# State-space stage of a four-layer image block on one core: stacked 3x3 taps, group 0 prepared beside attention, and an order written out per iteration

## The chip, the cores and the metric

The kernel runs on one core of one Trainium2 chip. The metric is device time in microseconds (us) of one execution. Five engines run their own instruction streams and meet at semaphores: TensorE (PE), VectorE (DVE), ScalarE (ACT), GpSimd (POOL) and SyncE (SP), which issues DMAs.

## The reference

Input and output are float32 images of 16 x 28 x 28 x 32. Four residual layers, each on a normalised image: window attention, a state-space layer, a triangle product, a recurrence. The change lies in the second:

```
x1 = grouped_1x1(gn(x), w1);  x1 = silu(conv3x3_depthwise(x1, dw))        # SAME padding
u, z = x1 @ in_proj                                                      # over the sequence of 784 pixels
u = silu(up[0:L]*c[0] + up[1:L+1]*c[1] + up[2:L+2]*c[2] + bias)          # causal, 3 taps
dt, B, C = x_proj(u);  delta = softplus(dt @ dt_proj + bias)
h_t = exp(delta_t * A[n]) * h_{t-1} + delta_t * u_t * B_t[n];  y = sum_n C_t[n] * h_t   # n = 0..7
y = (y + u * D) * silu(z);  x1 = layernorm(y @ out_proj) * gamma + beta
x = x + grouped_1x1(x1 * silu(grouped_1x1(gn(x), w2)), wout)
```

## The kernel before, in words

The image lies in X with 128 partitions, four images by 32 channels, and J = 4 groups of 784 columns (T = 784, HT = 392 a half). Weights are spread into block diagonals BD[128 x 128] for the four images (spread_weights, L1185). The 3x3 convolution is folded with w1 into nine such taps, U_CV.

Attention goes through 16 strips of 196 columns, software-pipelined over 18 steps: pe_att, act_att, dve_att and pool_att (L761, L547, L1230, L405), with steps 3 to 14 in hardware loops. dve_att(s) adds the projection of strip s-2 to X (L1253, semaphore x1_r). A strip takes 7.2 to 7.4 us.

Then gn_stats(1) and gn_apply(1) normalise all groups into XN, here with a border (30 x 30 a group), and the state stage starts. SSM_STEPS are six iterations i = -2 to 5. In iteration i each engine handles group f = i+2 (convolution, S1, u, z, x2), k = i+1 (delta, softplus, x_B, x_C), c = i (the eight states), m = i-1 (output, variance) and w = i-2 (scale, product wout, residual). The states of c:

- PE (pe_ssm): spread("B", n) and spread("C", n), L907, copy row n of B or C to all channels in PSUM, from three bf16 pieces in BCf. spread B n waits for the scan n-1 (v_s), spread C n for times_c(n-1) (v_c), since each has a single result place, pairs[0] and pairs[1]. All other products go to pairs[2] and pairs[3]; claim() waits until the last result there is read. conv is 18 full matmuls of 392 columns (L921), cut into pieces between the spreads; inner (L935) has 6.
- ACT (act_ssm): dA[n] = exp(A[n] * DL), L627, in four buffers, softplus in small steps in sp (L638 to L672), copies out of PSUM, and Silu. Functions of different tables need an ACT_TABLE_LOAD between them.
- DVE (dve_ssm): slot(n) is times_b (L1308), scan (L1315) and times_c(n-1) (L1328). DU = DL * US is L1380; y1 and y2 (L1362, L1367) make the gated output; L1350 shifts, L1373 is the residual.
- POOL (pool_ssm): add(n), L452, sums the eight hC into YA; split() (L460, L462) makes the bf16 pieces of B and C; L481 to L496 end the softplus in DL; L501 and L468 work on the layer norm.

Every engine works in program order, and waits are on semaphores: p_<name> that a product is there, c_<name> that it is read, v_dl, v_du, a_da, g_ya and so on. Engines reach the iterations in the same order, but nothing else ties them. In iteration -2 and -1 DVE has only DU of group 0 to do. While conv of group 0 runs, DVE prepares weights of the later layers (L1284 to L1299). After iteration 5 come gn_stats(2), gn_apply(2) and the triangle layer, then the recurrence.

## Time and profile before

| | us |
|---|---|
| median of 3 runs | 547.66 (546.55 to 547.82) |
| profiled execution | 548.09 |
| its span | 546.6 |
| PE busy | 387.7 (71%) |
| DVE busy | 373.4 (68%) |
| ACT busy | 289.5 (53%) |
| POOL busy | 229.6 (42%) |

Times in views are from the start of the span. The stages in it: loading and setup to 37, attention to 161, preparation of the state stage to 212, its four full iterations to 362, its tail to 393, triangle layer to about 470, recurrence to the end. A busy share is a mean over these; it says what bounds a stage only where the waits of that stage are read with it. PEclk is the granted TensorE clock, 1.00 for 2.4 GHz and 0.50 for 1.2 GHz.

### The profile page before, as it was taken

What the parts mean: (1) busy time and instruction counts of PE and PEld (TensorE: products, weight loads), DVE (VectorE), ACT (ScalarE), POOL (GpSimd) and SP (SyncE); (2) the same over time, 40 slices, a digit from 0 to 9 for tenths busy, and PEclk for the clock granted to TensorE, in tenths of its full rate; (3) what the DMA queues carried; (4) which work ended last, traced back from release to release, by engine and by line L of the source; (5) the groups of instructions that cost most, each with busy time, mean ns of one, the idle gap of its engine ahead of it and who ended that gap; (6) DMA issues with size and microseconds to landing.
All of it is one profiled execution on the core that took longest, in us unless ns stands there. A gap on an engine that the chain in (4) does not pass through costs nothing. (4 is left out here: it accounts for less than half of the span.)

```text
span 546.6 us, 10366 instructions
## 1 busy us (share of the span) xinstructions
PE 387.7 (71%) x3674; PEld 261.8 (48%) x3674; DVE 373.4 (68%) x679; ACT 289.5 (53%) x545; POOL 229.6 (42%) x205
## 2 busy tenths in 40 slices
PE   4169888899848898997995625423496181988885
PEld 3046666667635454453552201101385141987775
DVE  3797988888865003989988989974445776554443
ACT  4226888888850476837765720505476621333333
POOL 3616666777640090694795793483042000000000
PEclk9999999999997999898996755858597575999999
DMA  5100000000000000000000000000000000011111
GB/s 128 9 12 1 2 1 0 0 0 0 2 1 0 0 2 0 0 1 0 1 1 0 0 0 1 1 1 1 0 1 2 2 0 0 14 22 21 20 20 23
DMA packets 21571, 3.98 MB, mean 7 GB/s; under 512 B 19752, under 2 KB 21544, under 8 KB 21544
## 3 DMA queue, kind: packets, MB, share of 16 engines
q1 hardware_dynamic: 21416, 3.61, 4.0%
q8 instruction: 17, 0.28, 0.2%
q0 software_dynamic: 128, 0.01, 0.1%
q14 instruction: 10, 0.08, 0.1%
HBM read 2.00 MB, written 1.61 MB: 7 GB/s over the span
## 5 line engine op out<-in xcount | busy, mean ns | idle before, releaser
L452 POOL TENSOR_TENSOR YA<-YA,hC 128x784 f32<-128x784 f32 x28 | 53.7, 1919 | 42.2 <-DVE hC L1328 41.7
L425 POOL TENSOR_TENSOR Pr<-Pr,rc 128x392 f32<-128x392 f32 x64 | 52.3, 849 | 44.0 <-DVE rc L1263 44.0
L907 PE MATMUL pair<-BCf,sel 96*128 96x392 bf16 x128 | 39.8, 408 | 41.1 <-DVE Hs L1315 32.7
L1315 DVE TENSOR_TENSOR_SCAN Hs<-dA,pair 128x784 f32<-128x784 f32 x32 | 57.2, 1786 | 2.9 <-ACT dA L627 1.9
L921 PE MATMUL pair<-XN,BD 128*128 128x392 f32 x144 | 52.4, 513 | 5.9 <-DVE XN L1174 4.8
L907 PEld LDWEIGHTS pair<-BCf,sel 96*128 96x128 bf16 x128 | 11.0, 105 | 74.4 <-issue 71.7
L1241 DVE TENSOR_REDUCE mx<-pair 128x8 f32<-128x392 f32 x64 | 33.1, 558 | 14.0 <-PE pair L782 14.0
L570 ACT ACTIVATE PT<-pair 128x512 f32<-128x512 f32 x64 | 37.9, 592 | 7.9 <-PE pair L824 7.7
L921 PEld LDWEIGHTS pair<-XN,BD 128*128 128x128 f32 x144 | 28.0, 198 | 25.8 <-issue 9.8
L824 PE MATMUL pair<-ident,Pr 128*128 128x128 f32 x256 | 37.3, 285 | 3.5 <-POOL Pr L425 3.3
L1308 DVE TENSOR_TENSOR pair<-DU,pair 128x784 f32<-128x784 f32 x32 | 31.2, 974 | 10.6 <-PE pair L907 10.1
L576 ACT ACTIVATE Pr<-Ts 128x392 f32<-128x392 f32 x64 | 34.5, 541 | 5.6 <-DVE Ts L1247 4.9
L1380 DVE TENSOR_TENSOR DU<-DL,US 128x784 f32<-128x784 f32 x4 | 8.8, 2193 | 39.2 <-POOL DL L496 39.2
L782 PE MATMUL pair<-Km,Qw 32*64 32x196 f32 x512 | 31.3, 363 | 4.8 <-DVE Ts L1247 2.7
L824 PEld LDWEIGHTS pair<-ident,Pr 128*128 128x128 f32 x256 | 30.7, 146 | 8.2 <-POOL Pr L425 5.0
L1077 PE MATMUL pair<-XN,BD 128*128 (+1 forms) x168 | 25.5, 290 | 12.0 <-DVE XN L1174 12.0
L627 ACT ACTIVATE dA<-DL,Aneg 128x784 f32<-128x784 f32 x32 | 28.4, 938 | 9.3 <-POOL DL L496 9.3
L1089 PE MATMUL pair<-hst,BD 128*128 128x112 f32 x168 | 26.3, 294 | 9.4 <-DVE hst L1473 8.5
L1247 DVE TENSOR_TENSOR Ts<-pair,mx 128x392 f32<-128x392 f32 x64 | 32.9, 556 | 0.0
L1259 DVE TENSOR_REDUCE sm<-Pr 128x8 f32<-128x392 f32 x64 | 31.8, 539 | 0.0
L732 ACT ACTIVATE gates<-pair 128x224 f32<-128x224 f32 x28 | 10.0, 357 | 39.1 <-PE pair L1089 39.1
L460 POOL TENSOR_TENSOR BCf<-BCf 64x784 f32<-64x784 f32 x8 | 11.9, 1486 | 44.4 <-ACT BCf L644 44.4
(201 smaller groups left out, 944.9 us busy)
## 6 DMA issues: line engine op xcount, KB each, us to landing
XT<-in_x SPq DMA_DIRECT2D x4, 392.0 KB, 5.7
out<-Os SPq DMA_DIRECT2D x28, 56.0 KB, 1.8
NB<-in_L_conv_x_proj_w SPq DMA_DIRECT2D x4, 3.0 KB
DW<-in_L_conv_dw SPq DMA_DIRECT2D x4, 1.1 KB
vec<-in_L_conv_b_qkv POOLq DMA_DIRECT2D x3, 0.5 KB, 6.5
W<-in_L_conv_w_qkv SPq DMA_DIRECT2D x1, 48.0 KB
BL<-in_L_conv_bi SPq DMA_DIRECT2D x3, 0.5 KB
BL<-in_L_conv_bf SPq DMA_DIRECT2D x3, 0.5 KB
```

The lines of the kernel that those rows point to most:

```text
L425: eng.tensor_tensor(pg, pg, bcast(rc[:, g, :], 2, WT), ALU.mult).then_inc(pn_r, 1)
L452: eng.tensor_tensor(y, y, hC[:, n % NHC, :], ALU.add).then_inc(g_ya, 1)
L570: eng.activation(PT[:, g].rearrange("p a b q -> p (a b q)"), banks[5 + (par + 1 + g) % 2][:, :], ACT.Copy).then_inc(ring_r, 1)
L576: eng.activation(Pr[:, par, g, :, 0:WT], Ts[:, g, :, :], ACT.Exp).then_inc(exp_r, 1)
L782: ins = eng.matmul(banks[g][64 * half:64 * half + 64, 196 * pair:196 * pair + 196], Qw[C * g:C * g + C, par, 2 * pair + half, :], Km[C * g ...
L824: ins = eng.transpose(bk[:, P * k:P * k + P], pg, ident[:, :])
L907: ins = eng.matmul(SPREAD[s][:, HT * h:HT * h + HT], sel[:, n, :], upper(BCf[:, c % 2, s, HT * h:HT * h + HT]), start=True, stop=True)
L921: ins = eng.matmul(result("conv")[:, h, :].rearrange("p (y x) -> p y x", x=W), BD[:, U_CV + tap, :], img[:, f, y:y + 14, x:x + W], start=( ...
L1241: eng.tensor_reduce(mx[:, g, :], banks[g][:, 0:392].rearrange("p (m k) -> p m k", k=WT), AX.X, ALU.max).then_inc(max_r, 1)
L1247: eng.tensor_tensor(Ts[:, g, :, :], banks[g][:, 0:392].rearrange("p (m k) -> p m k", k=WT), bcast(mx[:, g, :], 2, WT), ALU.subtract).then_ ...
L1259: eng.tensor_reduce(sm[:, g, :], Pr[:, par, g, :, 0:WT], AX.X, ALU.add).then_inc(sum_r, 1)
L1315: eng.tensor_tensor_scan(Hs[:, n % 2, :], dA[:, n % NA, :], SPREAD[0], 0.0, ALU.mult, ALU.add).then_inc(v_s, 1)
```

## The change

What is computed stays. (1) The 3x3 taps: a normalised group lies in XP (two buffers, bordered). SP copies it by 12 DMAs of 32 partitions to SX, where three copies shifted by 0, 1 and 2 columns are stacked in 96 partitions for each of the four images. A half of the convolution is then 3 rows x 4 images of matmuls, 96 deep and 32 wide, with W3, in place of nine of 128 x 128. (2) Groups 0 and 1 are normalised within attention (after strip steps 10 and 12, which are unrolled on ACT and DVE), group 2 and 3 within iterations 0 and 1. (3) Group 0's convolution, u, delta and softplus are placed between the last steps of attention on PE, ACT, DVE; its results use pairs[0] and [1] (LEAD). The convolution, u and delta are handed on in halves. (4) Iterations run from 0 to 5, each with its order written out, for each engine; S1 has two buffers; y1 and y2 share yz, nt has one buffer instead of three, SP_W shares SP_U. (5) selections() moves from setup to step 15 of attention, later_weights() to iteration 4.

```diff
-        XN = sb("XN", [P, J * 30 * 30])
-        BD = sb("BD", [P, NU, P])
+        XN = sb("XN", [P, N])
+        XP = sb("XP", [P, 2, 30 * 30])
+        SX = sb("SX", [3 * C, G, 30 * 30])
+        W3 = sb("W3", [3 * C, 3, C])
+        BD = sb("BD", [P, U_CV, P])
...
+        LEAD = dict(conv=0, u=0, delta=1, xB=0, xC=1)
...
+            for b in range(J):
+                eng.wait_ge(xp_r, b + 1)
+                if b:
+                    eng.wait_ge(p_["conv"], count("conv", b - 1))
+                for x in range(3):
+                    for g in range(G):
+                        eng.dma_start(SX[C * x:C * x + C, g, 0:898], XP[C * g:C * g + C, b % 2, x:x + 898]).then_inc(s_sx, 16)
...
+            act_att(11, 1)
+            gn_ln(0, 2, 1)
+            gn_exp(0, 2)
+            for s in (12, 13, 14, 15):
+                act_att(s, s % 2)
...
+            silu_conv(0, 0)
+            silu_conv(0, 1)
+            def begin():
+                silu_u(0, 0)
+                silu_u(0, 1)
+                sp_abs(0, 0)
+                sp_abs(0, 1)
+            act_att(16, 0, begin)
+            sp_e(0)
+            sp_relu(0)
+            copy_bc(0, 0, "xB")
+            sp_u(0)
+            sp_l(0)
+            gn_ln(2, 3, 2)
+            copy_bc(0, 1, "xC")
+            sp_w(0)
+            gn_exp(2, 3)
+            silu_z(0)
+            silu_conv(1, 0)
+            silu_conv(1, 1)
+            decays(0, 0, 1, 2, 3)
...
+                elif i == 1:
+                    sp_abs(2, 0)
+                    sp_abs(2, 1)
+                    sp_relu(2)
+                    sp_e(2)
+                    sp_u(2)
+                    sp_u1(2)
+                    decays(1, 4)
+                    copy_bc(2, 0, "xB")
+                    decays(1, 5)
+                    sp_l(2)
+                    out_m(0)
+                    sp_w(2)
+                    copy_bc(2, 1, "xC")
+                    decays(1, 6)
+                    silu_conv(3, 0)
+                    silu_conv(3, 1)
+                    var_ln(0)
+                    decays(1, 7)
+                    var_exp(0)
+                    decays(2, 0, 1)
...
+            def conv(b, h):
...
+                for y in range(3):
+                    for g in range(G):
+                        ins = eng.matmul(row_groups(pairs[place("conv", b)][:, :, 0:HT], h)[g], W3[:, y, :],
+                                         rows[:, g, 14 * h + y:14 * h + y + 14, 0:W], start=(y == 0), stop=(y == 2))
...
+            conv(0, 0)
+            conv(0, 1)
+            pe_att(16, 0, early, late)
+            product("xB", 0, WBC[:, 0, :], US[:, 0, :])
+            pe_att(17, 1)
+            product("xC", 0, WBC[:, 1, :], US[:, 0, :])
+            gate(0)
+            conv(1, 0)
+            conv(1, 1)
...
+                if i == 0:
+                    spread("B", 0)
+                    spread("C", 0)
+                    inner(1, 0)
+                    inner(1, 1)
+                    spread("B", 1)
+                    x2(0)
+                    delta(1, 0)
+                    delta(1, 1)
+                    spread("B", 2)
+                    spread("C", 1)
+                    x_b(1)
+                    spread("B", 3)
+                    x_c(1)
+                    spread("C", 2)
+                    gate(1)
+                    spread("B", 4)
+                    spread("C", 3)
+                    conv(2, 0)
+                    spread("B", 5)
+                    spread("C", 4)
+                    conv(2, 1)
+                    spread("B", 6)
...
+            block_stats(0, 1)
+            dve_att(11, 1)
+            dve_att(12, 0)
+            padded(0, 1)
+            padded(1, 1)
+            for s in (13, 14, 15):
                 dve_att(s, s % 2)
+            selections()
+            dve_att(16, 0)
+            block_stats(2)
+            mk, rest = sp[:, SP_M, :], sp[:, SP_C, :]
+            eng.wait_ge(a_u, 1)
+            eng.scalar_tensor_tensor(rest, sp[:, SP_U, :], 1.0, sp[:, SP_E, :], ALU.subtract, ALU.subtract).then_inc(v_cc, 1)
+            dve_att(17, 1)
...
+                elif c is not None:
+                    slot(0)
+                    if i == 1:
+                        padded(3, 3)
+                    if i == 2:
+                        shift()
+                    outputs()
+                    slot(1)
+                    times_c(0)
+                    slot(2)
+                    times_c(1)
+                    slot(3)
+                    times_c(2)
+                    if i == 3:
+                        shift()
+                    slot(4)
+                    times_c(3)
+                    slot(5)
+                    times_c(4)
+                    if i == 2:
+                        residual()
+                    if i == 1:
+                        delta_u()
+                    slot(6)
+                    times_c(5)
+                    if i == 2:
+                        delta_u()
+                    slot(7)
+                    times_c(6)
+                    times_c(7)
+                    if i == 3:
+                        residual()
+                elif i == J:
+                    shift()
+                    outputs()
+                    later_weights()
+                    residual()
```

POOL's order in the changed kernel, which the diff writes out in the same way: iteration 0 is add 1, split(1, B), remainder (the former L481), add 2, plus_log (L486), add 3, delta (L491, L496), split(1, C), adds 4 to 7; iteration 1 is remainder, plus_log, add 1, split(2, B), add 2, delta, split(2, C), adds 3 and 4, scaled (L501), adds 5 to 7; iteration 2 is remainder, gated (L468), split(3, B), plus_log, add 1, delta, split(3, C), adds 2 to 4, scaled, adds 5 to 7; iteration 3 is add 1, gated, adds 2 and 3, scaled, adds 4 to 7. In iteration 4 PE has out_m, wout_w, var_m.

## Rows read from the trace of the kernel before

**Rows 1.** Stage windows: stretch, length, busy us per engine, PEclk, DMA share, GB/s.
```profile
60.00:150.00 90.00, 80.03 (x1486) 61.38 (x1484) 79.01 (x184) 75.20 (x184) 62.26 (x75) 1.00 0.00 1
212.50:249.40 36.90, 33.31 (x109) 16.56 (x107) 31.45 (x25) 25.47 (x29) 24.15 (x14) 0.95 0.00 0
249.40:288.00 38.60, 33.48 (x108) 17.14 (x108) 34.63 (x29) 26.78 (x31) 28.70 (x17) 0.96 0.00 1
288.00:327.90 39.90, 21.09 (x48) 7.08 (x48) 35.47 (x30) 21.20 (x25) 30.37 (x18) 0.61 0.00 0
327.90:362.30 34.40, 16.43 (x42) 4.71 (x42) 31.68 (x29) 9.22 (x10) 16.43 (x9) 0.65 0.00 1
```

**Rows 2.** Groups by line, DVE, 212:363: shapes, count, busy us, mean ns, idle before.
```profile
L1315 DVE TENSOR_TENSOR_SCAN Hs<-dA,pair 128x784 f32<-128x784 f32 x32 | 57.2, 1786 | 2.9 <-ACT dA L627 1.9
L1308 DVE TENSOR_TENSOR pair<-DU,pair 128x784 f32<-128x784 f32 x32 | 31.2, 974 | 10.6 <-PE pair L907 10.1
L1328 DVE TENSOR_TENSOR hC<-Hs,pair 128x784 f32<-128x784 f32 x28 | 26.6, 952 | 1.9 <-PE pair L907 1.8
L1380 DVE TENSOR_TENSOR DU<-DL,US 128x784 f32<-128x784 f32 x3 | 7.8, 2599 | 5.5 <-POOL DL L496 5.5
```

**Rows 3.** Timeline, head of the state stage: start us, us, engine, line, [idle before].
```profile
164.57 2.48 DVE L1174 TENSOR_SCALAR XN<-X,mv,rstd 128x784 f32<-128x784 f32 x4 [1.99 <-ACT rstd L539]
...
182.26 4.19 PE L935 MATMUL pair<-S,BD 128*128 128x392 f32 x12 [1.02 <-ACT S L681]
...
193.47 12.09 PE L921 MATMUL pair<-XN,BD 128*128 128x392 f32 x36 [1.00 <-ACT BCf L644]
...
205.68 0.98 DVE L1380 TENSOR_TENSOR DU<-DL,US 128x784 f32<-128x784 f32 x1 [33.70 <-POOL DL L496]
...
215.38 1.79 DVE L1315 TENSOR_TENSOR_SCAN Hs<-dA,pair 128x784 f32<-128x784 f32 x1 [1.86 <-ACT dA L627]
```

**Rows 4.** Timeline, last strips of attention.
```profile
152.53 0.90 PE L835 MATMUL pair<-PT,Vst 128*32 128x49 f32 x64 [1.28 <-ACT PT L570]
...
154.42 1.91 DVE L1152 BATCH_NORM_STATS2 stats<-X 128x6 f32<-128x392 f32 x4
...
160.64 0.42 DVE L1253 SCALAR_TENSOR_TENSOR X<-pair,vec,X 128x196 f32<-128x196 f32 x1 [2.66 <-PE pair L806]
```

**Rows 5.** Timeline, ACT and POOL in group 0's softplus.
```profile
193.35 1.28 ACT L647 ACT_TABLE_LOAD   x1
...
194.64 0.86 ACT L647 ACTIVATE sp<-sp 128x784 f32<-128x784 f32 x1
...
201.78 1.84 POOL L491 TENSOR_TENSOR sp<-sp 128x784 f32<-128x784 f32 x1 [0.32 <-ACT sp L672]
```

**Rows 6.** Timeline, DVE at the end of setup.
```profile
30.35 2.42 DVE L1185 TENSOR_TENSOR BD<-W,bd 128x2176 f32<-128x2176 f32 x1
...
33.30 3.35 DVE L1221 CAST sel<-ident 32x1024 bf16<-32x1024 f32 x3
...
37.01 1.04 DVE L1241 TENSOR_REDUCE mx<-pair 128x8 f32<-128x392 f32 x2
```

**Rows 7.** Waits, 60:150: who, for whom, us in total, times, longest.
```profile
DVE mx L1241 <- PE pair L782: 10.6, 18, 0.8
```

**Rows 8.** Timeline, SP's queue in setup.
```profile
24.70 0.53 SPq L299 DMA_DIRECT2D W<-in_L_conv_Wox  x1
```

**Rows 9.** DMA issues: count, KB each, median us to landing.
```profile
out<-Os SPq DMA_DIRECT2D x28, 56.0 KB, 1.8
```

**Rows 10.** Timeline, DVE's preparation of later weights, first and last instruction.
```profile
166.97 0.15 DVE L1286 TENSOR_SCALAR vec<-vec 128x1 f32<-128x1 f32 x1
...
171.40 0.58 DVE L1299 TENSOR_TENSOR WZ<-wzs,maskz 64x128 f32<-64x128 f32 x2
```

**Rows 11.** Timeline, DVE in the tail of the state stage.
```profile
374.57 0.97 DVE L1373 TENSOR_TENSOR X<-X,pair 128x784 f32<-128x784 f32 x1 [6.35 <-PE pair L891]
```

**Rows 12.** Timeline, PE in iteration 3, a product.
```profile
337.37 2.98 PE L891 MATMUL pair<-y,BD 128*128 128x392 f32 x4 [1.05 <-DVE y L1367]
```

More of the change, by code:

```diff
@@ new lines, in silu_z, with silu_x2, sp_abs @@
+            def silu_z(b):
+                eng.wait_ge(p_["z"], b + 1)
+                eng.activation(halves(ZS[:, b, :]), result("z", b), ACT.Silu).then_inc(c_["z"], 1)
+            def silu_x2(b):
+                eng.wait_ge(p_["x2"], b + 1)
+                eng.activation(halves(X2[:, b, :]), result("x2", b), ACT.Silu).then_inc(c_["x2"], 1)
+            def sp_abs(k, h):
+                eng.wait_ge(p_["delta"], 2 * k + h + 1)
+                if k and h == 0:
+                    eng.wait_ge(v_dl, k)
+                eng.activation(sp[:, SP_E, columns(h)], result("delta", k)[:, h, :], ACT.Abs, bias=vec[:, V_DTB:V_DTB + 1]).then_inc(c_["delta"], 1)
@@ L888, in product @@
-            def product(name, w, rhs):
-                claim(name)
+                    n, d = last[-1]
+                    if not (d == b and (n, name) in (("conv", "u"), ("u", "delta"))):
+                        eng.wait_ge(c_[n], count(n, d))
+                    if n == "delta":
+                        eng.wait_ge(a_m, d + 1)
+                elif place(name, b) >= 2:
+                    eng.wait_ge(ring_r, 6 * NS)
+                    eng.wait_ge((x1_r, ao_r)[place(name, b) - 2], NS)
@@ L955, in pe_ssm @@
-                spread("B", 3)
-                conv(4, 6)
-                spread("C", 2)
-                if w is not None:
-                    eng.wait_ge(g_nt2, w + 1)
-                    product("wout", BD[:, U_WO, :], nt[:, 2, :])
-                conv(6, 8)
-                spread("B", 4)
-                conv(8, 11)
-                spread("C", 3)
-                if m is not None:
-                    eng.wait_ge(c_["out"], m + 1)
-                    product("var", VB[:, :], sq[:, :])
```

836 lines of the change are left out of this document (537 added, 299 removed).

## The prediction

> **What bounds the kernel now.** First read the stage windows [rows 1], busy time per engine, then PEclk. In the four iterations of the state stage (212.5 to 362.3 us, 149.8 us) DVE works 31.5 of 36.9, 34.6 of 38.6, 35.5 of 39.9 and 31.7 of 34.4 us. PE looks as busy in the first two, but that is work DVE does not wait for: the groups of DVE's instructions [rows 2] show 10.1 us of waiting for the spreads over 32 products, 1.9 us for dA, 5.5 us for DL. So there DVE is the bound. One state needs L1308, L1315 and L1328: 0.97 + 1.79 + 0.95, starts 3.57 us apart when nothing waits, 28.6 us per group.
>
> Second, read the timeline ahead of it [rows 3]. DVE's last instruction of attention is at 160.6 [rows 4]; the first DU is at 205.68 after 33.70 us idle, and the first scan at 215.38. These 54 us are one chain through group 0: statistics, 36 records of the 3x3 convolution at a cold clock, S1, u, delta, softplus, DL, and then group 1's convolution (12.09 us at 193.47) standing on PE in front of the first spread. That head is the largest thing that can be removed.
>
> **The head of the state stage.** Eighteen full-array matmuls take 12.09 us, 0.67 each [rows 3]. The new conv has 12 matmuls a half, each 32 columns wide and 96 rows deep, four of them to different column groups. The nearest row is L835 [rows 4]: 64 records, 32 matmuls on 128*32 tiles, 49 columns, in 0.90 us; at 0.67 us for 392 columns one such matmul alone would take 0.084, 32 of them 2.7. So at least three run side by side. A half then costs between 3 x 0.67 = 2.0 and 8.0/3 = 2.7 us; I take 2.0, as the 0.90 contains start and end.
> The Trainium skill (TensorE: Matmul & The Clock Gate, Measured speedup vs the span model) reports 2.38 times for three column tiles, which at four would make a half 2.5 us by proportion; the sum would lose about 1 us. The row decides for the full overlap, and 2.7 stays the upper end.
>
> Now walk the new order, on the clock of the old trace. PE finishes the av at 152.53 + 0.90 = 153.4 [rows 4]. conv(0,0) and (0,1) end at 155.6 and 157.6. ACT has the Silu table loaded (1.28, [rows 5]) by 155.3, S1 by 156.2 and 158.1. pe_att(16) with inner in it: inner has 3 matmuls a half (12 records took 4.19, [rows 3]), so 2.1 each; transposes, inner(0,0), project, transposes, inner(0,1) end at 164.8, delta(0,1) at 166.3, av(15) at 167.2. ACT: AO at 167.9, table load and sp_e 170.1, relu and xB copy 171.8, sp_u 172.6, table load and sp_l 174.8, xC copy and small Ln 175.8, table load and sp_w 178.1, table load, silu_z and silu_conv(1) 181.3, table load and dA(0) 183.5 (each full-width operation about 0.86, [rows 5]). DVE in parallel: L1253 of the last strip now waits behind a_u and runs at 173.7 instead of 160.6, mk and rest end 179.8 (one may stand behind a POOL split), DL 180.8, DU 181.8, times_b 182.8. conv(1) waits for x1_r 16, 174.2 to 178.2, and spread B 0 follows in time. The first scan starts at 183.5 instead of 215.4: -31.9 us. Unknown: ACT alone carries four table loads between AO and dA, so any slip on it counts fully; bounds -28 and -33.
>
> **Attention and setup.** selections() leaves setup: L1221 cost 3.35 and stood directly before the first L1241 at 37.01, and L1185 shrinks from 2176 to 1024 columns, 2.42 to about 1.2 [rows 6]; W3 and split copies cost about 0.7. Some 4 us less ahead of the first maximum, but Km and the cold PE are close behind; I take -3 (bounds -4 and -1). In the drain the selections stand where DVE now idles, and cost nothing; if the cover were gone, 3.7. Into the steady part go two groups of statistics (1.91, [rows 4]) plus aggregation, two padded (0.62 each as a quarter of the 2.48 of L1174, [rows 3], possibly behind a POOL multiply), and on ACT two tiny operations with two table loads, 3 us. DVE has 10.6 us of waits in 90 us [rows 7], 0.9 a strip, to swallow them; behind each stand maxima and exponentials that PE and POOL wait for. I take +4.5 (bounds +1 and +8). Net +1.5. The memset of XP, half of what XN's was, falls into POOL's idle time (62.3 busy of 90, [rows 1]).
>
> **The 12 copies a group.** SP issues a DMA in 0.53 and every 0.57 us [rows 8]; 12 give 6.8, and the last lands some 1.8 after its issue as the 56 KB stores do [rows 9]: 8.6 us. Group 0 has more than three strips of attention to hide them, group 1 from 157.6 to 174.2. Group 2 can start only after padded(2), near 190, and PE reaches conv(2,0) near 199: just hidden. Group 3: 220 to 231, hidden. SP's queue holds nothing else until the stores of the last stage. Upper bound for a transfer, if 32 partitions take half the rate: 17 us.
>
> **The four iterations.** DVE per group keeps 28.6. Iteration 0 (from scan 0, was 34.0): 27.6 + padded 1.3 + group 3's statistics 1.2 + DU 2.6 (mean of L1380, [rows 2]: 0.98 alone at 205.68, [rows 3], and 2.6 in the loop, beside a POOL operation of 1.84, [rows 5]) + 1.5 of small waits = 34.2, no gain. Iteration 1 (38.6): outputs() now lies between scan 0 and times_b 1 and so covers the 1.0 us wait for the spread, the 1.7 wait for DL changes into one of about 1.9, since POOL does remainder, plus_log, add, split, add, delta in a row (1.84 each), padded costs 1.3, DU lands on POOL less surely: 37.6. Iteration 2 (39.9): DL two us earlier, slot 1 covered, shift without a POOL neighbour: 36.6. Iteration 3 (34.4): the shift (1.3) enters, residual and slot waits leave: 32.9. Sum -5.8 (bounds +4 and -12; each saving is a fraction of a wait, each of the twelve SBUF-only DVE operations may cost 1.6 more or less). conv leaves PE 8 us a group that nobody waited for in iterations 0 and 1: nothing directly. ACT in iteration 1 has, counted in the new order, 24 us of operations (27 or so of 0.86 and halves of it) and nine table loads, 11.5: 35.4 of 37.6. It is nearly a second bound, but dA(4) to dA(7) come out several us before their scans when I walk it, so I cost it at nothing; without that cover 2 to 6 us.
>
> **The tail.** later_weights (166.97 to 171.98, [rows 10]: 5.0 us) moves behind the last outputs(). There DVE idled 6.35 us in front of L1373 (374.57, [rows 11]), and wout now follows out on PE at once, so the residual comes out level or a little earlier: -0.5. If the cover fails, residual(2) is late, and with it var, Ln, rstd: +1. Everything behind is unchanged.
>
> **Sum.** -31.9 + 1.5 - 5.8 - 0.5 = -36.7. The profiled execution took 548.1 (span 546.6 and 1.5 around it), so 511.4; the median of the runs shown is 0.4 lower: 511.0.
>
> **Rivals.** (a) Column groups do not overlap for 392-column streams (four different moving reads at once). Then a half costs 8.0: 12 us more in the chain of group 0, 8.5 for group 1 (2 x 6 less 3.6 of slack before spread B 0), 6 for each of four halves in the loop where the spread behind has 2.1 us of room, 24: 555.5, slower than before. It decides the sign only if a half costs over 7.1 us, an overlap under 1.15; L835's row speaks against. 0.04.
> (b) The clock. Rows 1 show 0.95 and 0.96 in iterations 0 and 1 and 0.61 and 0.65 in 2 and 3, where PE had little to do; a product of two halves at the low level took 2.98 us [rows 12], where two matmuls at 0.67 [rows 3] make 1.34. Without 8 us of convolution, iterations 0 and 1 might run at 1.2 GHz as well: conv and inner halves of 4 us in front of spreads with 2.1 us of room, seven times 1.9, 13 us: 524. For: PE's work falls to 33.5 - 12.1 + 4.0, 25 of 38 us. Against: attention holds 1.00 with pauses in every strip. 0.14. The Trainium skill (TensorE: Matmul & The Clock Gate, HAM oscillation — how this bites in real kernels) warns that pauses between bursts throw the clock back; the granted clock behind the 1.0 us waits of iteration 3 agrees.
> (c) The copies take 17 us each group: conv(2,0) 8 late, conv(3,0) 6 late, PE stands and with it the spreads: 525. 0.09.
> (d) In-order ACT becomes the bound of iterations 0 and 1, or attention stretches by the full 8: 517 to 520. 0.13.
> (e) No DVE and POOL collisions and no DL wait: -12 in the loop: 504.8. 0.10.
> The forecast, 506 to 516, keeps 0.50.
>
> **Range and chances.** 503 to 526 takes in (b) to (e) with their edges and leaves out (a) and the tails of both sides. About 0.3% is what a measurement can tell from no change; all cases but (a) are far beyond it: faster 0.95, same 0.01, slower 0.04.
>
> **What would show it.** First scan between 180 and 188 us; the wait of DVE on DL ahead of the state stage gone from 33.7 to a few us; 24 conv records of a half within 2.0 to 2.7 us; iterations of 33 to 38 us with DVE busy over 0.93; PEclk near 1.0 in the first two; attention's last strip 1 to 3 us later in the stretch before the drain; L1373's counterpart after later_weights at the same distance from the last outputs(). Wrong it would be if a convolution half costs over 4, if PE waits for SP's copies in the loop, or if spreads wait behind products of 3 us.

## The result, and the profile after

| | before | after |
|---|---|---|
| median of the runs, us | 547.11 (4 runs, 546.47 to 547.82) | 523.57 (4 runs, 521.22 to 526.34) |
| ratio after to before | | 0.957, 95% interval 0.952 to 0.962 |
| profiled execution, us | 548.1, span 546.6 | 523.5, span 521.7 |
| first scan of the state stage | 215.38 | 183.46 |
| end of the last times_c of iteration 3 | 362.29 | 333.16 |
| first write of XR | 390.66 | 368.02 |
| from there to the end of the span | 155.9 | 153.7 |

The change makes the kernel 23.5 us faster. The forecast was 511.0 with a range of 503 to 526: the direction and the range held, but the time lies outside the 506 to 516 that were given a chance of one half, and a third of the expected gain is missing. The table tells in which stretch it went. Up to the first scan 31.9 us are gained, against 31.9 - 1.5 = 30.4 expected. From there to the end of the four iterations before took 146.9 us and after takes 149.7: a loss of 2.8 where a gain of 5.8 was forecast. From there to XR before took 28.4 and after 34.9: a loss of 6.5 where a gain of 0.5 was forecast. These two stretches, 8.6 and 7.0 us off, are what the experiments are about.

The stage windows of after, one for each iteration, answer to [rows 1] (stretch, length, busy us of each engine, PEclk, DMA share, GB/s):

```profile
183.40:217.90 34.50, 28.34 (x121) 11.47 (x119) 31.64 (x29) 30.50 (x38) 23.81 (x14) 0.90 0.18 41
217.90:259.20 41.30, 32.51 (x121) 13.34 (x122) 33.44 (x29) 30.44 (x36) 29.26 (x17) 0.79 0.15 34
259.20:299.60 40.40, 22.70 (x63) 8.48 (x61) 33.79 (x30) 28.23 (x33) 30.45 (x18) 0.79 0.00 1
299.60:333.10 33.50, 17.43 (x42) 6.14 (x42) 31.33 (x29) 10.16 (x11) 16.48 (x9) 0.65 0.00 0
```

DVE works 31.6 of 34.5 and 31.3 of 33.5 us in the first and the last, but only 33.4 of 41.3 and 33.8 of 40.4 in the two between: 14.5 us in which the engine that should be the bound stands. The groups of DVE's instructions, 183.4 to 333.2 us, say behind whom; they answer to [rows 2]:

```profile
L1705 DVE TENSOR_TENSOR_SCAN Hs<-dA,pair 128x784 f32<-128x784 f32 x32 | 57.2, 1786 | 1.1
L1698 DVE TENSOR_TENSOR pair<-DU,pair 128x784 f32<-128x784 f32 x32 | 31.1, 973 | 3.7 <-PE pair L1198 3.0
L1718 DVE TENSOR_TENSOR hC<-Hs,pair 128x784 f32<-128x784 f32 x28 | 26.6, 950 | 14.5 <-PE pair L1198 14.5
L1753 DVE TENSOR_TENSOR DU<-DL,US 128x784 f32<-128x784 f32 x3 | 6.5, 2182 | 0.0
```

The three instructions of a state cost what they did. The 5.5 us of waiting for DL are gone, and in front of the scans only 1.1 is left. But in front of times_c there are 14.5 us of waiting for L1198, the spreads, and a spread is a short product that stands in PE's queue behind something else. So the question is what stood ahead of it.

The head came as walked. PE, then DVE, from the timeline of after, beside [rows 3, 4]:

```profile
154.55 4.14 PE L1130 MATMUL pair<-SX,W 96*32 96x392 f32 x48
```

```profile
172.71 1.62 DVE L1658 SCALAR_TENSOR_TENSOR sp<-sp 128x784 f32<-128x784 f32 x1 [8.60 <-ACT sp L746]
...
183.46 1.79 DVE L1705 TENSOR_TENSOR_SCAN Hs<-dA,pair 128x784 f32<-128x784 f32 x1
```

The line of PE is both halves of group 0's convolution, 24 matmuls (two records each) in 4.14 us: 2.07 a half, where 2.0 was taken. Group 1's two halves take 4.16 us from 174.81 on. DVE's longest idle time in the head is 8.60 us in front of the first remainder, waiting for ACT; the scan comes at 183.46.

### The profile page after: what moved, and what is told of

The parts are those of the page before. It is cut to its first block, busy times and chain, and to the rows that moved or that the text cites. A ratio compares the mean times of both kernels' runs of the same rounds, so it can differ in the third digit from the quotient of the medians.

```text
span 521.7 us, 10477 instructions
## 1 busy us (share of the span) xinstructions
PE 365.1 (70%) x3722; PEld 242.5 (46%) x3722; DVE 385.2 (74%) x687; ACT 304.9 (58%) x571; POOL 224.7 (43%) x201
## 4 chain that ended last, share of the span: by engine, by line
DVE 29%; PE 26%; ACT 19%; issue 15%; SPq 5%; POOL 4%; DMA 1%; DVEq 1%; POOLq 0%; ACTq 0%
PE pair L1435 4%; DVE pair L1698 4%; DVE Hs L1705 3%; PE pair L993 3%; SPq L317 3%; PE pair L1130 3%; DVE Ts L1599 2%; PE pair L1198 2%; PE pair L1046 2%; ACT PT L647 2%; PE pair L1114 2%; POOL Pr L451 2%; DVE hC L1718 2%; ACT gates L943 2%; POOL pp L591 1%
## 5 line engine op out<-in xcount | busy, mean ns | idle before, releaser
L451 POOL TENSOR_TENSOR Pr<-Pr,rc 128x392 f32<-128x392 f32 x64 | 54.3, 880 | 41.3 <-DVE rc L1615 41.3
L1198 PE MATMUL pair<-BCf,sel 96*128 96x392 bf16 x128 | 38.5, 405 | 33.1 <-DVE Hs L1705 26.2
L1593 DVE TENSOR_REDUCE mx<-pair 128x8 f32<-128x392 f32 x64 | 32.9, 555 | 14.6 <-PE pair L993 14.6
L1198 PEld LDWEIGHTS pair<-BCf,sel 96*128 96x128 bf16 x128 | 10.7, 106 | 69.2 <-issue 67.0
L647 ACT ACTIVATE PT<-pair 128x512 f32<-128x512 f32 x64 | 37.7, 592 | 7.9 <-PE pair L1035 7.6
L1718 DVE TENSOR_TENSOR hC<-Hs,pair 128x784 f32<-128x784 f32 x28 | 26.6, 950 | 14.5 <-PE pair L1198 14.5
L653 ACT ACTIVATE Pr<-Ts 128x392 f32<-128x392 f32 x64 | 34.5, 541 | 3.1 <-DVE Ts L1599 2.6
L1599 DVE TENSOR_TENSOR Ts<-pair,mx 128x392 f32<-128x392 f32 x64 | 32.9, 555 | 0.0
L1901 DVE SCALAR_TENSOR_TENSOR prods<-gates 128x112 f32<-128x112 f32 x28 | 7.7, 276 | 33.1 <-ACT gates L943 33.1
L445 POOL TENSOR_TENSOR Km<-Ks,mask 128x784 f32<-128x784 f32 x16 | 24.1, 1505 | 12.3 <-ACT Ks L639 12.3
L1435 PEld LDWEIGHTS pair<-hst,BD 128*128 128x128 f32 x168 | 21.5, 196 | 13.8 <-DVE hst L1914 13.5
```

Source lines behind the costliest of these rows:

```text
L451: eng.tensor_tensor(pg, pg, bcast(rc[:, g, :], 2, WT), ALU.mult).then_inc(pn_r, 1)
L647: eng.activation(PT[:, g].rearrange("p a b q -> p (a b q)"), banks[5 + (par + 1 + g) % 2][:, :], ACT.Copy).then_inc(ring_r, 1)
L653: eng.activation(Pr[:, par, g, :, 0:WT], Ts[:, g, :, :], ACT.Exp).then_inc(exp_r, 1)
L1198: ins = eng.matmul(SPREAD[s][:, HT * h:HT * h + HT], sel[:, n, :], upper(BCf[:, c % 2, s, HT * h:HT * h + HT]), start=True, stop=True)
L1435: ins = eng.matmul(zb[k], BD[:, U_M + k, :], hst[:, 1 - par, :], start=False, stop=True, skip_group_check=True)
L1599: eng.tensor_tensor(Ts[:, g, :, :], banks[g][:, 0:392].rearrange("p (m k) -> p m k", k=WT), bcast(mx[:, g, :], 2, WT), ALU.subtract).then_ ...
```

## Experiments

The ratio of each kernel is to the kernel before on the same chip, the interval is 95%. A difference is given by the medians and, where it says so, by the ratios, which stand nearer to each other for kernels that ran on different chips. Several kernels build on each other; each text says on which.

### The yardstick: the changed kernel again

> The changed kernel as it is, as the yardstick for the other runs of this chip. All theories: 521 to 526 us, ratio to the kernel before near 0.957; first scan at 183.5 us, wait of DVE in front of times_c(2) of iteration 1 near 4.8 us, wait at the end of iteration 2 near 6.0 us, the W scaling of later_weights() near 6.8 us.

Measured: 523.53 us, ratio 0.956 (0.955 to 0.958), span 521.2. First scan at 181.58. All three stalls are there (5.4 and 1.3 us in iteration 1, 6.0 at the end of iteration 2, 6.80 for the scaling). Two things differ. Attention's last reciprocal comes at 153.68 where the first profile had 155.55; the granted clock from 120 to 135 us was 0.89 here and 0.78 there. From that reciprocal to the first scan both executions take 27.9 us, as do all kernels below that leave this part as it is. And in iteration 0 the granted clock stayed at 1.00 where the first profile had 0.90, and DVE's two waits of 0.93 and 1.38 us are gone; the iteration took 34.5 us in the first profile and 32.5 in this one. Iteration 1 gives the 2 us back (43.5 us here, 41.3 there). So differences of about 2 us in attention and in a single iteration come with the same code; a single iteration is compared below with that of an execution whose iteration 0 ran alike.

### The tail: later_weights() against POOL's memset

In the timeline of after, DVE first and then POOL (whose L519 is a multiplication of the layer norm):

```profile
336.50 2.49 DVE L1740 TENSOR_TENSOR yz<-yz,ZS 128x784 f32<-128x784 f32 x1
338.92 0.14 DVE L1676 TENSOR_SCALAR vec<-vec 128x1 f32<-128x1 f32 x1
338.98 6.80 DVE L1677 TENSOR_SCALAR W<-W 128x128 f32<-128x128 f32 x1
...
350.53 0.97 DVE L1747 TENSOR_TENSOR X<-X,pair 128x784 f32<-128x784 f32 x1
...
357.75 0.98 DVE L1819 TENSOR_TENSOR nt<-cS,rs 128x784 f32<-128x784 f32 x1 [3.31 <-ACT rs L813]
```

```profile
335.60 2.56 POOL L519 TENSOR_TENSOR nt<-nt,X 128x784 f32<-128x784 f32 x1 [0.50 <-DVE nt L1728]
...
339.63 6.07 POOL L580 MEMSET XR<- 128x7168 f32 x1
```

A scaling of 128 columns takes 6.80 us and ends at 345.78, as the memset does at 345.70 (it starts beside the shorter memset of Zc, 338.10 to 339.69). residual(2) (L1747) comes at 350.5; var, the root on ACT and the last normalisation wait for it. The memset stood in the same place before, in the idle time of DVE that the prediction meant to fill; POOL's timeline of the kernel before:

```profile
367.85 6.07 POOL L473 MEMSET XR<- 128x7168 f32 x1
```

DVE idled 6.35 us in front of 374.57 [rows 11]: from 368.2 on, the very time of the memset. Two kernels try the lock, one by moving DVE's work, one by moving POOL's.

e1_weights_early:

```
                 block_stats(2)
...
+                later_weights()
                 eng.wait_ge(a_u, 1)
...
                 elif i == J:
                     shift()
                     outputs()
-                    later_weights()
                     residual()
```

> later_weights() runs in DVE's idle of 8.6 us ahead of the first softplus remainder (163.9 to 172.7 us) instead of beside POOL's memsets of Zc and XR at 339 us. Theory (the tail lost its 6 us because DVE's scaling of W stood against POOL's memset for 6.80 us, and residual(2), var, the square root and the last normalisation are late by it): the scaling takes 0.2 us again, residual(2) comes at about 344 instead of 350.5, and the whole kernel is 6 to 7 us shorter than the changed kernel, 517. Rival (the tail is set by wout's product at the low clock or by another chain, and later_weights() only fills idle time): below 1 us of difference. First scan unchanged at 183.5 by both.

Measured: 519.05 us, ratio 0.947 (0.946 to 0.949), 4.5 us shorter than the yardstick (by the ratios 4.9). From e1's timeline, DVE:

```profile
163.68 0.22 DVE L1662 TENSOR_SCALAR W<-W 128x128 f32<-128x128 f32 x1
...
172.34 1.62 DVE L1678 SCALAR_TENSOR_TENSOR sp<-sp 128x784 f32<-128x784 f32 x1 [3.71 <-ACT sp L746]
...
346.37 0.97 DVE L1747 TENSOR_TENSOR X<-X,pair 128x784 f32<-128x784 f32 x1 [7.74 <-PE pair L1114]
```

The scaling takes 0.22 us. In the head the work is wholly covered: 3.71 us are left of the 8.60, and the first scan is at 183.10, again 27.9 us behind attention's last reciprocal. residual(2) moved only from 350.5 to 346.4, because it now waits 7.74 us for wout on PE: a second bound lay 4 us behind the first (in after, wout had left PE at 346.7). So 6 to 7 was too much; to have the routine out of the tail is worth 4.5. This run alone doesn't separate the slow scaling from the 5 us of work that went with it; the next one does.

e6_memset_late, which leaves later_weights() where the change put it:

```
                         eng.wait_ge(g_ya, (DS - 1) * J)
+                        eng.wait_ge(c_["wout"], J - 1)
                         for buf in (Zc, XR):
```

> POOL zeroes Zc and XR only behind residual(2); later_weights() stays in iteration 4. Theory (lock: DVE's W scaling takes 6.80 us only because POOL's memset runs beside it): the scaling takes 0.2 us, later_weights() 5.0 us in all as before the change, residual(2) near 345, 4 to 4.5 us shorter than the changed kernel, 519, as with the weights moved ahead. Rival 1 (the scaling is slow by itself there): no change. Rival 2 (the memset of 6.1 us then stands against DVE's statistics or nt and costs there what it saved): 522 to 525.

Measured: 519.53 us, ratio 0.950 (0.947 to 0.953), 4.0 us shorter than the yardstick (by the ratios 3.7). DVE and POOL of e6:

```profile
339.10 0.21 DVE L1678 TENSOR_SCALAR W<-W 128x128 f32<-128x128 f32 x1
...
352.69 0.97 DVE L1820 TENSOR_TENSOR nt<-cS,rs 128x784 f32<-128x784 f32 x1 [1.91 <-ACT rs L814]
353.70 2.30 DVE L1729 TENSOR_SCALAR nt<-nt,vec 128x784 f32<-128x784 f32 x1
```

```profile
349.51 6.07 POOL L581 MEMSET XR<- 128x7168 f32 x1
```

The same instruction at the same place takes 0.21 us without the memset beside it, and residual(2) comes at 346.86 with the whole routine still in front of it: the lock is shown from both sides, and it accounts for 3.7 us of the tail. The memset now catches another tensor_scalar, the shift at 353.70: 2.30 us instead of 0.69, done at 356.00, with the memset at 355.58. The tensor_tensor at 352.69 lies inside the same memset and takes its usual 0.97. What stands against the memset is the tensor_scalar and not the tensor_tensor, although both have all their operands in SBUF. Beside an operation of POOL that reads SBUF the tensor_tensor is slow too: y2 (L1740) at 336.50 takes 2.49 us beside POOL's multiplication of 335.60 to 338.16, and 0.97 elsewhere. The Trainium skill (SBUF — State Buffer, "SBUF: two separate sides") says that a DVE instruction in a 2-port mode takes the port pair that it shares with GpSimd and waits for the whole of the other's instruction, and that one with two SBUF inputs does so only against a GpSimd operation that reads SBUF. The three rows agree, if the tensor_scalar ran in such a mode, which no row shows directly.

### Iteration 1: the copies or the claim

In the timeline of after PE stands 3.37 us ahead of conv(3, 0), and the prediction had named SP's copies as what could be late there. PE, then ACT:

```profile
229.66 0.51 PE L1198 MATMUL pair<-BCf,sel 96*128 96x392 bf16 x2 [0.88 <-DVE Hs L1705]
233.54 3.51 PE L1130 MATMUL pair<-SX,W 96*32 96x392 f32 x24 [3.37 <-ACT BCf L738]
...
238.40 4.15 PE L1130 MATMUL pair<-SX,W 96*32 96x392 f32 x24
```

```profile
230.54 1.28 ACT L758 ACT_TABLE_LOAD   x1
231.83 0.86 ACT L758 ACTIVATE sp<-sp 128x784 f32<-128x784 f32 x1
232.59 0.80 ACT L738 ACTIVATE BCf<-pair 96x784 f32<-96x784 f32 x1
```

The releaser named is not a DMA but ACT's copy of xC(2), which ends at 233.4. conv(b) and xC(b - 1) share PSUM pair 2, and claim() lets the convolution wait until that product is read; x_c(2) itself had left PE at 225.9. Both convolution halves then run at the low clock (3.5 and 4.15 us instead of 2.1), and each stands in front of a spread.

e2_xc_early:

```
                     copy_bc(2, 0, "xB")
+                    copy_bc(2, 1, "xC")
                     decays(1, 5)
                     sp_l(2)
                     out_m(0)
                     sp_w(2)
-                    copy_bc(2, 1, "xC")
```

> In iteration 1 ACT copies xC of group 2 out of PSUM directly behind xB (at about 227 us instead of 232.6). Theory A (conv(3, 0) claims the PSUM pair of xC(2), so it waited for this copy at the end of a row of ACT's work, and SP's copies had landed at 230.2 before that): conv(3, 0) starts at 230.2 instead of 233.5, DVE's wait in front of times_c(2) falls from 4.8 to between 1 and 1.6 us, the kernel is 3 to 4 us shorter, 520. Theory B (the 12 copies of group 3 land only then; the copy on ACT was in time): no difference, 523.5.

Measured: 518.91 us, ratio 0.946 (0.943 to 0.948), 4.6 us shorter than the yardstick (by the ratios 5.9). PE of e2:

```profile
227.49 0.51 PE L1198 MATMUL pair<-BCf,sel 96*128 96x392 bf16 x2 [0.88 <-DVE Hs L1705]
227.92 2.18 PE L1130 MATMUL pair<-SX,W 96*32 96x392 f32 x24
...
231.50 2.18 PE L1130 MATMUL pair<-SX,W 96*32 96x392 f32 x24
```

Theory A holds: the convolution follows the spread at once, so the copies had landed. The wait was expected to shrink to 1 to 1.6 us; in fact it went to zero, as did the one behind conv(3, 1), since both halves now take 2.18 us. The iteration takes 36.6 instead of 43.5 us in the yardstick, 6.9 less; iteration 2 takes 42.9 instead of 41.2, which gives some of it back.

### The end of iteration 2: a knot of orders

ACT, PE and DVE of after:

```profile
291.93 0.95 ACT L769 ACTIVATE dA<-DL,Aneg 128x784 f32<-128x784 f32 x1 [4.44 <-DVE Hs L1705]
...
294.19 0.82 ACT L718 ACTIVATE ZS<-pair 128x784 f32<-128x784 f32 x1
```

```profile
295.06 2.98 PE L1163 MATMUL pair<-XP,BD 128*128 128x392 f32 x4 [7.05 <-ACT ZS L718]
```

```profile
298.73 0.97 DVE L1718 TENSOR_TENSOR hC<-Hs,pair 128x784 f32<-128x784 f32 x1 [5.98 <-PE pair L1198]
```

Decay 3 of group 3 reuses the buffer of state 7 of group 2 and so waits for DVE's last scan. Behind it in ACT's queue stand a table load of 1.28 us and silu_z(3), x2(3) on PE claims the pair that silu_z(3) reads, and the last spread stands behind x2(3) on PE. DVE waits for itself.

e4_z_early:

```
-                    decays(3, 0, 1, 2, 3)
+                    decays(3, 0, 1, 2)
                     silu_z(3)
                     silu_x2(3)
+                    decays(3, 3)
```

> At the end of iteration 2 ACT runs silu_z(3) and silu_x2(3) before the fourth decay of group 3, which waits for scan(2, 7), instead of behind it. Theory (a knot of orders: scan(2, 7), then decay, table load, silu_z(3), x2(3) on PE, spread C 7, times_c(7)): DVE's wait of 6.0 us in front of the last times_c of iteration 2 falls to 0 to 1.5 us, the kernel is 4.5 to 6 us shorter, 518.5. Rival (PE's products at the low clock hold that spread back anyway, 3 us of x2 after its turn): 2 us or less.

Measured: 518.02 us, ratio 0.945 (0.944 to 0.947), 5.5 us shorter than the yardstick (by the ratios 6.0). PE and DVE of e4:

```profile
290.15 2.98 PE L1164 MATMUL pair<-XP,BD 128*128 128x392 f32 x4 [1.66 <-ACT ZS L718]
```

```profile
294.16 0.97 DVE L1719 TENSOR_TENSOR hC<-Hs,pair 128x784 f32<-128x784 f32 x1 [0.99 <-PE pair L1199]
```

The wait falls from 5.98 to 0.99 us, the iteration from 40.4 to 35.4 (its iterations 0 and 1 are those of after, 34.5 and 41.3 us). The product still runs at the low clock, 2.98 us, and can cost no more than the 0.99 us that are left, so the rival is out.

### The three together

> The three edits together: weights early, xC copied early, Silus of group 3 before its fourth decay. Theory (three separate stalls, each on DVE's path, with no common cover): the three differences add, 4.5 + 4.6 + 5.5 = 14.6 us, so 509 us (507 to 511). Rival (one of them hides another, as when PE's higher clock moves the last one): 511 to 516.

Measured: 509.67 us (506.85 to 512.04), ratio 0.931 (0.928 to 0.935). 14.6 us were expected and 13.9 are found; by the ratios it is 13.8 where the three alone add up to 16.8. So they add, or nearly: the time is within the expected 507 to 511, and the rival's 511 to 516 begins where the interval ends. The stage windows of this kernel:

```profile
183.70:218.10 34.40, 28.32 (x121) 11.47 (x119) 31.56 (x28) 30.42 (x38) 23.75 (x14) 0.90 0.18 41
218.10:253.40 35.30, 27.93 (x121) 12.22 (x122) 33.32 (x29) 29.89 (x36) 27.51 (x16) 0.90 0.18 40
253.40:291.10 37.70, 23.38 (x63) 8.27 (x61) 35.66 (x30) 29.04 (x33) 32.17 (x19) 0.79 0.00 0
291.10:324.10 33.00, 16.04 (x42) 5.78 (x42) 31.33 (x29) 9.84 (x11) 16.58 (x10) 0.66 0.00 0
```

34.4, 35.3, 37.7 and 33.0 us; the forecast had 34.2, 37.6, 36.6 and 32.9, so the sum agrees in part because two of its terms miss in opposite ways. From the last times_c (324.1) to XR (352.4) are 28.3 us, as in the kernel before (28.4), and 1.4 less than in e1, whose wout took 2.95 us at the low clock where it takes 1.55 here.

### Undoing the early preparation

u1_prepare_late, on the changed kernel:

```
-            block_stats(0, 1)
-            dve_att(11, 1)
-            dve_att(12, 0)
-            padded(0, 1)
-            padded(1, 1)
-            for s in (13, 14, 15):
+            for s in (11, 12, 13, 14, 15):
                 dve_att(s, s % 2)
+            block_stats(0, 1)
+            padded(0, 1)
+            padded(1, 1)
             selections()
```

and on ACT gn_ln(0, 2, 1) and gn_exp(0, 2) behind strip 15 in the same way.

> One part of the change undone: statistics, square root and padded images of groups 0 and 1 come at the end of attention, behind strip 15, and no longer between strips 10 and 13; the rest of the change stays. Theory (the early preparation is what lets convolution 0 start right behind the last product of attention; it costs attention 6 us and saves statistics, root, image and 12 copies on the chain): attention's last reciprocal near 149 us, then 2.3 us of statistics, 3.1 us of root with table loads, 0.7 us of image, 9 us of copies, convolution 0 at 164 instead of 154.6, first scan 8 to 10 us later than 183.5, kernel 532. Rival (the copies and statistics overlap the drain, as PE still has two strips to finish): first scan within 3 us, kernel 522 to 526.

Measured: 536.26 us, ratio 0.979 (0.975 to 0.983), 12.7 us longer than the yardstick (by the ratios 12.1). PE of u1:

```profile
148.04 0.90 PE L1045 MATMUL pair<-PT,Vst 128*32 128x49 f32 x64 [1.28 <-ACT PT L647]
164.08 6.66 PE L1129 MATMUL pair<-SX,W 96*32 96x392 f32 x48 [15.14 <-DMA SX<-XP]
```

The last product of attention's strip 15 comes 5.8 us earlier (153.84 in after), and then PE stands 15.14 us, for the chain of statistics, root, image and copies, and both halves together take 6.66 us instead of 4.14. First scan at 195.1, 11.6 us later than in after, where 8 to 10 were expected. From its first maximum to its last reciprocal attention takes 117.5 us, as in the kernel before (117.2), where after takes 123.6 and the yardstick 121.6. About half of the change's gain hangs on this one part, net of the 4 to 6 us that it costs attention.

### The copies: 24 instead of 12

d1_24_copies, on the combined kernel (the waits on s_sx count 32 a copy in place of 16):

```
-   eng.dma_start(SX[C * x:C * x + C, g, 0:898], XP[C * g:C * g + C, b % 2, x:x + 898]).then_inc(s_sx, 16)
+   for o in (0, 449):
+       eng.dma_start(SX[C * x:C * x + C, g, o:o + 449], XP[C * g:C * g + C, b % 2, x + o:x + o + 449]).then_inc(s_sx, 16)
```

> The combined kernel with each of the 12 copies of a group cut into two of half the length: the same bytes with twice the issues. Theory (a group's copies are bound by SP's issuing, 0.62 us each, and with 12 of them land just before PE needs them): 24 take about 16 us, conv(2, 0) is 6 to 7 us late, conv(3, 0) 5 us late, PE's clock falls there as well, 10 to 16 us longer than 509.7: 520 to 526. Rival (the bytes set the time, 12 x 112 KB): no change, 510.

Measured: 527.9 us, ratio 0.962 (0.957 to 0.966), 18 us longer than the combined kernel (by the ratios 17). SP's queue in iteration 0, first of after, then of d1:

```profile
189.65 7.50 SPq L389 DMA_DIRECT2D SX<-XP  x12
```

```profile
191.60 15.85 SPq L390 DMA_DIRECT2D SX<-XP  x24
```

PE and DVE of d1:

```profile
208.90 4.15 PE L1132 MATMUL pair<-SX,W 96*32 96x392 f32 x24 [9.25 <-DMA SX<-XP]
```

```profile
213.85 0.98 DVE L1700 TENSOR_TENSOR pair<-DU,pair 128x784 f32<-128x784 f32 x1 [10.11 <-PE pair L1200]
```

12 issues take 7.50 us, 24 of half the size 15.85: SP's issuing sets the time of the copies and not their bytes. In after, conv(2, 0) starts 9.2 us behind the first issue (8.6 were taken) and waits 1.23 us for it. The rival of slow copies had priced 17 us a group at 14 us for the kernel; 15.85 cost 17 to 18, more than the 10 to 16 expected: DVE waits 10.11 us in iteration 0 and 9.28 in iteration 1 in front of the spread, since behind each wait the convolution halves run at 4.15 us.

### wout in its own PSUM pair

m2_wout_pair, on the combined kernel:

```
-        PAIR = dict(B=0, C=1, conv=2, u=2, delta=2, xC=2, xB=3, wout=3, out=3, var=3, z=3, x2=3)
+        PAIR = dict(B=0, C=1, conv=2, u=2, delta=2, xC=2, xB=3, wout=2, out=3, var=3, z=3, x2=3)
```

> The combined kernel with the product wout in PSUM pair 2, which is free after xC(3), so that var no longer waits for residual(2). Theory: in the tail var starts when wout has left PE, at about 336.2 instead of 337.4 us, and in iterations 2 and 3 nothing changes: 1 to 2 us shorter than 509.7, 508. Rival (var then runs at the low clock, 3.0 us instead of 1.55, and takes back what it starts earlier): within 0.5 us.

Measured: 504.53 us (503.98 to 506.18), ratio 0.921 (0.918 to 0.923). It is 5.1 us shorter than the combined kernel by the medians, 5.7 by the ratios, 3.7 by the profiled spans (508.1 and 504.4). Its tail:

```profile
332.51 1.84 PE L1115 MATMUL pair<-nt,BD 128*128 128x392 f32 x4
334.44 1.55 PE L1115 MATMUL pair<-sq,VB 128*128 128x392 f32 x4
```

wout follows out directly and var follows wout; in the combined kernel they started at 334.67 and 337.38. From the last times_c to XR are 25.6 us instead of 28.3, 2.7 gained, more than the 1 to 2 expected, because wout no longer waits for ACT to read out. The four iterations are the same (140.3 and 140.4 us). Of the 3.7 us between the spans, 2.7 are these, 0.2 lie ahead of the first scan and 0.7 behind XR, where the edit changes nothing; what the medians show beyond that the traces don't explain. This is the fastest version: 43 us below the kernel before, 19 below the changed one.

### conv(2) one spread later

m3_conv2_late, on m2:

```
-                    conv(2, 0)
                     spread("B", 5)
                     spread("C", 4)
+                    conv(2, 0)
...
```

and so for conv(2, 1) and inner(2, 0).

> As m2_wout_pair, and in iteration 0 both halves of conv(2) and inner(2, 0) one spread later. Theory (conv(2, 0) waited 1.2 us for the last copy, the granted clock fell to 0.5 and both halves took 3 and 4 us, so DVE waited 0.9 and 1.4 us): both waits go, 2 us shorter than m2_wout_pair, 506. Rival (silu_u(2, 0) and the decays behind it on ACT come late by the same spread, or the clock falls all the same): equal to m2_wout_pair or up to 3 us longer.

Measured: 510.4 us, ratio 0.932 (0.929 to 0.936), 5.9 us longer than m2 (by the ratios 6.5): the theory was wrong. PE of m3:

```profile
198.86 0.51 PE L1199 MATMUL pair<-BCf,sel 96*128 96x392 bf16 x2 [3.38 <-DVE Hs L1706]
...
200.46 4.15 PE L1131 MATMUL pair<-SX,W 96*32 96x392 f32 x24
```

Nothing waits for the copies, but PE now stands 3.38 us for DVE's scan, the clock falls all the same (0.50 granted from 202 to 206 us, as in m2), and a half takes 4.15 us. DVE's waits in iteration 0 grow from 0.9 and 1.4 to 2.3, 1.3 and 3.1 us. In the profiled executions the four iterations take 145.0 us instead of 140.3. So the low clock there doesn't need the wait for the copy.

What PE did just before doesn't decide it alone either. In the 16 us from the first scan on, PE was busy 12.10 us in m2, whose clock then fell, and 12.09 in the yardstick, whose clock held; counted in stretches of 2 us the two agree to 0.01, with 1.00 granted in all of them. The next 2 us of m2, then of the yardstick (columns as above):

```profile
199.51:201.51 2.00, 2.00 (x20) 0.47 (x12) 2.00 (x2) 1.99 (x3) 2.00 (x2) 0.65 0.03 8
```

```profile
197.58:199.58 2.00, 2.00 (x22) 0.52 (x14) 2.00 (x2) 1.99 (x3) 2.00 (x2) 1.00 0.03 8
```

What differs is the moment. Among the kernels that leave iteration 0 and the copies as they are, the clock held where the first scan came at 181.45 to 182.12 us or at 195.08, and fell where it came at 183.10 to 183.91 or at 179.12. No run here varies the moment alone, so this stays a suggestion.

### Order within a convolution half

e5_serial_tiles, on the changed kernel:

```
-                for y in range(3):
-                    for g in range(G):
+                for g in range(G):
+                    for y in range(3):
```

> The 12 matmuls of a convolution half in the order group by group, three taps behind each other in the same 32 columns, instead of tap by tap over the four column groups. Theory (the short half of 2.07 us needs neighbours in the queue that stand in different column groups): half 0.49 us each laid end to end where neighbours share columns, about 5 to 6 us a half, first scan 10 us later or more, the kernel 25 to 50 us longer than the changed one, about that of the kernel before. Rival (PE overlaps them in whatever order, or the half is short because it has 12 and not 18 matmuls): a half stays at 2 to 2.7 us and the time at 523.

Measured in a single execution: 527.56 us, span 525.8 (521.2 and 521.7 for the changed kernel). PE of e5:

```profile
150.97 6.98 PE L1130 MATMUL pair<-SX,W 96*32 96x392 f32 x48
```

3.49 us a half instead of 2.07. The first scan lies 31.5 us behind attention's last reciprocal (152.0 and 183.5) instead of 27.9 (155.6 and 183.5). So the order matters and the overlap of column groups is real, but two forecasts of this run were too dark: neighbours of one column group don't fall back to end to end (5 to 6 us a half), and the kernel pays some 4 us and not 25. The 3.6 us of the head are what the trace shows; the kernel's own 4 rest on one execution, where those of the changed kernel lie between 521.2 and 526.3.

### The square root between strips

e8_no_table, on the changed kernel:

```
-   link(eng.activation(lnv[:, j0:j1], mv[:, j0:j1, 1], ACT.Ln, bias=epsc[:, 0:1]))
+   link(eng.activation(lnv[:, j0:j1], mv[:, j0:j1, 1], ACT.Ln if turn > 1 else ACT.Exp, bias=epsc[:, 0:1]))
```

> In the strips of attention ACT computes an Exp in place of the Ln of the first group normalisation, so the variance of groups 0 and 1 comes out wrong and two table loads (1.28 us each) between strips 11 and 12 are not there. Theory (the attention stretch of +6 us is made by ACT's 3.1 us beside the two padded images and statistics, and PE's clock falls to 0.78 over that stretch): attention's last reciprocal 3 to 4 us earlier than 155.5, first scan near 180, kernel near 520. Rival (DVE's own 4.3 us of statistics and images make the stretch, ACT's loads lie beside them): less than 1.5 us.

The kernel leaves out the logarithm of the variance, so its output is not that of the reference. Measured: 521.55 us, ratio 0.953 (0.951 to 0.956), 2 us shorter than the yardstick; the two intervals overlap (0.955 to 0.958), so these 2 us are at the edge of what the runs can tell. Attention takes 119.3 us from its first maximum to its last reciprocal, against 120.2 to 123.7 in the eleven profiled executions with the loads between the strips, and the first scan is at 179.1 (183.5 in after, 181.6 in the yardstick). The windows from 120 to 135 us, of after and then of e8 (columns as above):

```profile
120.00:135.00 15.00, 12.50 (x210) 9.42 (x210) 12.85 (x27) 11.04 (x27) 9.28 (x11) 0.78 0.10 24
```

```profile
120.00:135.00 15.00, 13.05 (x224) 9.61 (x212) 14.06 (x32) 12.10 (x32) 10.72 (x12) 1.00 0.24 54
```

DVE works 14.1 instead of 12.9 us there and the clock stays at 1.00 (0.89 in the yardstick). So the two table loads with what follows from them take between 1 and 4 us of attention. In this execution the iterations give them back: the clock fell in iteration 0, and the four take 152.9 us instead of the yardstick's 150.5. The kernel's 2 us are therefore not a clean price of the loads. The rest of attention's 4 to 6 us would be DVE's own statistics and images; that is argued from their place and was not tried.

## Why the prediction was right, and where not

| term | forecast | after | combined kernel |
|---|---|---|---|
| up to the first scan | -30.4 | -31.9 | -31.7 |
| four iterations | -5.8 | +2.8 | -6.5 |
| to XR | -0.5 | +6.5 | -0.1 |
| behind XR | 0 | -2.2 | -0.2 |
| span | -36.7 | -24.9 | -38.5 |

**The head** was right by its steps, and 1.3 us better than walked: from attention's last reciprocal to the first scan the kernel before took 61.1 us and after takes 27.9, 33.2 less, where 31.9 had been walked. A convolution half takes 2.07 us (2.0 taken, 2.7 the upper end), so the rival of column groups that don't overlap is out. The walk through PE, ACT and DVE named 183.5 for the first scan, and 185.0 with attention's 1.5; it came at 183.46, and at 181.58 in another execution of the same code.

**Attention and setup** came to the sum by two misses that cancel. The first maximum is at 31.92 instead of 37.01, -5.1 where -3 was taken (the row of it shows no wait, so Km and PE were not close behind), and from there to the last reciprocal attention takes 123.6 instead of 117.2 us, +6.4 where +4.5 was taken. The sum is +1.3 against the +1.5 taken, which is luck. The early preparation is the cause, since u1 without it takes 117.5; the two table loads and the clock of 0.78 in the stretch behind them are a part of it.

**The copies** were right in size (9.2 us against 8.6, and issuing sets it). Their cover was 1.2 us short for group 2; for group 3 it was just enough: conv(3, 0) followed its spread at once in e2, and waits 0.34 us for the last copy in the combined kernel.

**The iterations.** The step that failed is the one sentence that group 3's copies are "hidden" from 220 to 231 us: it asked when the convolution's data is there and not when its PSUM pair is free. claim() makes conv(3, 0) wait for the reading of xC(2), and that copy stood in ACT's queue behind a table load, a logarithm, two copies of out, another load and an exponential. The prediction costed the order on ACT "at nothing" with 2 to 6 us without the cover, after walking ACT for its decays alone, and the same blind spot holds the second stall: silu_z(3) behind a decay that waits for the last scan. Removing them gave 4.6 and 5.5 us in the kernel, and then the iterations take 140.4 us where the forecast's four add up to 141.3 (5.6 less than before, not the 5.8 of its sum). The rest of that part held: 28.6 a group, DU at 2.2 us (2.6 taken), the DL wait gone in after and 0.9 us in the combined kernel. All three signs that the prediction named as showing it wrong appeared in the loop: convolution halves of 4.0 to 4.15 us, PE waiting 1.23 us for SP's copies, and spreads behind products of 3 us.

**The clock.** The rival of a falling clock is half right: 0.90 and 0.79 in iterations 0 and 1, not near 1.0. Its 524 lies beside the measured 523.57, but that is luck: it counted no stall of ACT's queue and none in the tail. In iteration 1 the low clock of the convolution is a follower of the wait: with xC copied early both halves take 2.18 us. In iteration 0 it fell in some executions and not in others of the same code, and cost 2.3 us of waits in DVE's row, which the other executions lost in iteration 1; what decides it stays open.

**The tail.** The step of the tail that failed is the cover. "6.35 us idle" [rows 11] was read on DVE's row alone; in that same time POOL ran its memset of 6.07 us, and an instruction of the moved routine stands against it. The 5.0 us of work became 11.6 (338.92 to 350.51). "If the cover fails: +1" was too small since it priced only the 5.0 us. And "wout now follows out on PE at once" was wrong too: both used one PSUM pair, so wout stood 1.72 us until ACT had read out, which m2 shows by taking it away.

**Behind XR** nothing was changed, and 2.2 us are gained in the first profile. With the same code behind that point, other kernels took 153.6 us (d1) to 155.9 (e2) from there to the end, so the 2.2 us are within what one execution differs from another.

## What to carry to other kernels

When work is moved into an engine's idle time, read the partner's row of the same stretch as well: idle on DVE beside a long POOL instruction is not free for a tensor_scalar whose operands lie in SBUF, as the 6.80 us here. When a queue is written out by hand, walk every claim of a shared buffer to the instruction that frees it and to what stands ahead of that one in its own queue; both stalls in the loop were one line too late on an engine that was not the bound. And cover a chain of many small copies by counting issues, not bytes.

## What the runs showed of the hardware that had not been expected

- A tensor_scalar on 128 columns took 6.80 us beside a POOL memset and 0.21 without it, while a tensor_tensor of 784 columns inside the same memset kept its 0.97 us.
- Twelve matmuls of 96x32 on four column groups take 2.07 us tap by tap and 3.49 us group by group, where twelve full-array matmuls would take 8.0 (0.67 each in the kernel before), so a good part of the overlap survives even where neighbours share columns.
- The granted clock in iteration 0 differed between two executions of the same kernel (1.00 and 0.90) whose first scans lay 1.9 us apart, after 16 us of the same work of PE at 1.00.
